# Eight expert blocks moved into the last attention batch, with their rows and biases fetched there

## What is computed

```python
qkv = (x @ W_qkv + b_qkv).reshape(B, S, 3, H, hd)
attn = softmax(einsum('bqhd,bkhd->bhqk', q, k) / sqrt(hd))
attn_out = einsum('bhqk,bkhd->bqhd', attn, v)
gate = softmax(x @ W_gate + b_gate)
top_g, top_i = top_k(gate, 2)
combine = sum(one_hot(top_i, E) * top_g)
expert_out = einsum('bsd,edf->bsef', x, W_experts) + b_experts
moe_out = einsum('bsef,bse->bsf', expert_out, combine)
return attn_out + moe_out        # added to x by the caller
```

## Time and profile before

| what | before |
|---|---|
| median of 3 runs | 1406.44 us (1406.14 to 1407.71) |
| profiled execution, span | 1410.6 us |
| PE busy | 1305.5 us (93%) |
| DVE busy | 967.5 us (69%) |
| ACT busy | 903.4 us (64%) |
| POOL busy | 363.8 us (26%) |
| DMA | 219.83 MB, mean 156 GB/s |

### The profile page before, as it was taken

One profiled execution on the slowest core, in us unless ns is written; L12 is line 12 of the kernel. 1 busy time (PEld: TensorE's weight loads), 2 busy tenths in 40 slices (PEclk: granted clock), 3 DMA queues, 4 the chain that ended last, 5 costly groups with the idle time before them and its releaser, 6 DMA issues. The chain is left out here.

```text
span 1410.6 us, 27655 instructions
## 1 busy us (share of the span) xinstructions
PE 1305.5 (93%) x7744; PEld 994.7 (71%) x7745; DVE 967.5 (69%) x2143; ACT 903.4 (64%) x1888; POOL 363.8 (26%) x572
## 2 busy tenths in 40 slices
PE   4998999999888899999999999999988779999996
PEld 4967888888666567776777776777764358777775
DVE  4256888888678888888888888888876524433332
ACT  4123545444358799999999999999987723333332
POOL 0002222222200011312102131110010047777765
PEclk9998999999899999999999999999996789999998
DMA  5006777776665257564545745556479377867763
GB/s 163 1 1 228 265 268 264 251 266 246 231 164 150 38 135 161 134 165 85 145 128 138 188 84 123 143 144 164 104 166 309 131 191 140 146 124 134 139 129 52
DMA packets 113387, 219.83 MB, mean 156 GB/s; under 512 B 28489, under 2 KB 36809, under 8 KB 111155
## 3 DMA queue, kind: packets, MB, share of 16 engines
q1 hardware_dynamic: 84064, 173.47, 40.9%
q0 software_dynamic: 26624, 42.04, 17.3%
q10 hardware_dynamic: 2643, 3.65, 0.8%
HBM read 86.82 MB, written 77.73 MB: 117 GB/s over the span
## 5 line engine op out<-in xcount | busy, mean ns | idle before, releaser
L225 PE MATMUL banks<-parts 128*128 128x512 f32 (+6 forms) x1108 | 443.0, 400 | 32.7 <-DVE parts L1334 7.4
L227 PE MATMUL banks<-parts 128*128 128x512 f32 (+6 forms) x1108 | 423.5, 382 | 0.0
L226 PE MATMUL banks<-parts 128*128 128x512 f32 (+6 forms) x1108 | 422.9, 382 | 0.0
L1549 DVE TENSOR_REDUCE plain<-banks 128x1 f32<-128x512 f32 x512 | 339.5, 688 | 82.9 <-PE banks L1053 69.8
L774 ACT ACTIVATE banks<-banks,plain 128x512 f32<-128x512 f32 x512 | 346.2, 683 | 15.4 <-DVE plain L1549 15.1
L781 ACT ACTIVATE plain<-banks 128x1024 f32<-128x1024 f32 x256 | 266.9, 1043 | 39.6 <-PE banks L1075 38.4
L225 PEld LDWEIGHTS banks<-parts 128*128 128x128 f32 (+1 forms) x1108 | 214.2, 193 | 85.4 <-issue 24.2
L227 PEld LDWEIGHTS banks<-parts 128*128 128x128 f32 (+1 forms) x1108 | 213.0, 192 | 40.8
L226 PEld LDWEIGHTS banks<-parts 128*128 128x128 f32 (+1 forms) x1108 | 214.4, 194 | 30.8
L1075 PE MATMUL banks<-parts 104*128 104x512 f32 x512 | 179.8, 433 | 6.2 <-ACT plain L781 4.7
L1053 PE MATMUL banks<-parts 96*128 96x512 f32 x512 | 184.9, 413 | 0.7 <-ACT banks L774 0.3
(11 more groups left out here) (180 smaller groups left out, 1506.8 us busy)
## 6 DMA issues: line engine op xcount, KB each, us to landing
parts<-parts SPq DMA_DIRECT2D x384, 128.0 KB, 2.4
parts<-h_turned SPq DMA_DIRECT2D x46, 512.0 KB, 6.5
experts_split<-parts SPq DMA_DIRECT2D x32, 512.0 KB, 4.1
h_turned<-parts SPq DMA_DIRECT2D x32, 512.0 KB, 2.9
parts<-experts_split SPq DMA_DIRECT2D x8, 2048.0 KB, 9.8
plain<-in_x_dram SPq DMA_DIRECT2D x32, 256.0 KB, 4.1
plain<-in_L_ffn_W_experts_dram SPq DMA_DIRECT2D x32, 256.0 KB, 4.1
out_dram<-plain SPq DMA_DIRECT2D x32, 256.0 KB, 2.8
```

Source lines behind the costliest of these rows:

```text
L225: pe.matmul(out, stat[0], mov[0], start=first, stop=False)
L226: pe.matmul(out, stat[0], mov[1], start=False, stop=False)
L227: return pe.matmul(out, stat[1], mov[0], start=False, stop=last)
L1549: dve.tensor_reduce(nmx[:, k, t:t + 1], bank[SB[t]][:], AX.X, ALU.max, negate=True).then_inc(q["f_max"], 1)
```

## The change

In heads 5 to 15 of the last batch the table `FILLED` stands in for `STEP`. The empty `D` slots take the halves of 8 early expert blocks (token `x`, all with expert 0). The tokens `r`, `g` and `l` are the rows' transposes (PE), high part (ACT) and low part (DVE). DVE adds the bias (`early_sum`), POOL multiplies by the gate (`weigh`). POOL gathers blocks 0 to 7 and then 8 to 15 in this batch. The expert stage computes blocks 8 to 71, with gathers 8 blocks ahead; the adds of the first 8 blocks are still made after the attention's outputs have landed. Biases for block 8 to 15 are loaded ahead from a copy in DRAM. Since rows and biases take areas of experts 7 and 6, those two are loaded when blocks 8 to 15 are done, and 3, 4 and 5 as heads 12, 14 and 16 are turned.

```diff
+            "begun": {"pe": "n@1 T2@2 S0 S1 r S2 Pa Pb T0@1 S3 D0",
+                      "act": "t2@2 E3@1 g E0 o t0@1 E1 E2",
+                      "dve": "s@1 n@1 m0 l m1 D1@1 m2 m3"},
...
+        FILLED_FROM = 5
...
-            for token in STEP[KINDS[k % 4]][engine].split():
+            for token in (FILLED if last and k >= FILLED_FROM else STEP)[KINDS[k % 4]][engine].split():
...
+                    if last and of is b and half[0] in "NV":
+                        if what[0] == "D":
+                            yield "x", of, early_half(head, what[1])
+                        continue
...
+                if r == 0:
+                    sp.dma_start(be_early[:], b_exp[bass.ds(e, 1)].broadcast_to([P, D])).then_inc(q["in_wk"], 16)
...
-                    load_expert(3)
...
+                    sp.dma_start(be_first, be_dram.broadcast_to([P, NE * D])).then_inc(q["in_wq"], 16)
+                    sp.wait_ge(q["f_t_full"], T * (NH * b + 12))
+                    load_expert(3)
+                    sp.wait_ge(q["f_t_full"], T * (NH * b + 14))
                     load_expert(4)
-                    sp.wait_ge(q["f_t_full"], T * (NH * b + 12))
+                    sp.wait_ge(q["f_t_full"], T * (NH * b + NH))
+                    sp.wait_ge(q["v_full"], NT + U)
                     load_expert(5)
...
+            for i in range(U, 2 * U):
+                added(i)
+            sp.wait_ge(q["m_tr"], U)
+            load_expert(7)
+            sp.wait_ge(q["m_sum"], U)
+            load_expert(6)
...
+                if i >= 2 * U:
+                    pool.wait_ge(q["m_tr"], i - 2 * U + 1)
+                elif i >= U:
+                    pool.wait_ge(q["h_tr"], NT + i - U + 1)
...
+            def weigh(i):
+
+                pool.wait_ge(q["x1_part"], NT + i + 1)
+                pool.tensor_scalar(rows[i], rows[i], lst[:, i, 1:2], None, ALU.mult).then_inc(q["x1_ready"], 1)
...
+            for i in range(U):
+                fetch(U + i)
+                if i == 4:
+                    attended(B - 1, 0)
+                if i:
+                    weigh(i - 1)
             attended(B - 1, 1)
+            weigh(U - 1)
...
             for i in range(NB):
-                if i + 4 < NB:
-                    fetch(i + 4)
+                if 5 <= i < U + 5:
+                    fetch(2 * U + i - 5)
+                if 2 * U <= i < NB - U:
+                    fetch(i + U)
                 add(i)
...
+            def early_turn(i, k):
+
+                pe.wait_ge(q["f_pt"], ((B - 1) * NH + k - 2) * 2 + 2)
+                pe.wait_ge(q[in_rows(i)], rows_before(i) + 16)
+                for c in range(C):
+                    last = pe.transpose(bank[0][:, c * P:(c + 1) * P], rows[i][:, c * P:(c + 1) * P], ident[:])
+                last.then_inc(q["h_tr"], 1)
...
                         elif what[0] == "T":
+                            if held:
+
+                                pe.wait_ge(q["hT_ready"], NT + held)
+                                held = 0
...
-                    await_ge(dve, "m_done", i - 3)
+                    if part != "first" or k >= 4:
+                        dve.wait_ge(q["m_done"], i - 3)
```

155 lines of the change are left out of this document (118 added, 37 removed), and 6 rows, old and new, of the table FILLED.

## The result

The changed kernel takes 1397.28 us (median of 10 runs, 1392.4 to 1401.23), the one before 1406.38 (median of 10 in the same comparison). The ratio is 0.9935, 95% interval 0.9916 to 0.9953: 9.1 us less, where 19.1 were forecast. The time lies in the forecast's range; the gain is half of what was said.

What follows compares the result with a forecast made beforehand. The last batch was held to be bound by PE's lowered clock, the expert stage by POOL's queue, with PE nearly as tight. Terms -3.5 - 21.6 + 5 + 1 = -19.1 us took 1406.4 to 1387; range 1374 to 1402.

Steps and rivals of the forecast that it cites:

- The expert stage: POOL's queue behind the landing: 237.5 us before loads, 21.6 less than 259.1, with 8.9 of waits for late rows gone.
- rival 1: Expert stage shrinks with its blocks, 64 for 72: 28.8 us less, loads hidden, 1374 us; chance 12%.
- Loads of experts 7 and 6: 4 MB loaded inside the expert stage, sharing DMA packets one for one with gathers and adds: 5 us more, bounds 0 and 13.4.
- near 0: Price of the expert stage's two loads if DMA turns let many small descriptors by; 1382 us in the end.
- Dense adds: Some 10 expert-stage adds without a gather, 1.9 us apart, might be slowed by DMA: 1 us more, bounds 0 and 7.
- rival 2: DMA binds the expert stage: loads cost 13.4 us in full and dense adds 7, 1402 us; chance 15%.
- The landing: Last attention output's landing follows the load's issue, not the batch's end: 0.7 of the 4.2 us gained is lost.
- The tail: Head 15 to last output: two faster products with V give 3.3 us, a half block costs 1.4: 1.9 less of 19.4.
- The last batch: Heads 5 to 14 at 57.0 instead of 59.3 us, 2.3 less, and the tail 1.9 less: 4.2 less.
- What batch 6 doesn't have is 8 x 0.5 = 4.0 on PE.: Last batch, heads 5 to 14: full batch 6 takes 52.3 us; eight blocks' transposes add 4.0, all on the path.
- Rival 3: Last batch: turned scores wait for transposes and both splits, 14.2 us instead of 4.7, 1397 us; chance 10%.
- Rival 4: Last batch: PE still pauses and filled matmuls run at half clock, 27 us more, 1414 us; chance 8%.

Runs made afterwards that it cites:

- e7_noload: The changed kernel with the loads of experts 7 and 6 left out but for 16 columns each: 1393.90 us, ratio 0.9911 to before.
- after: The changed kernel itself in its first profile, against the kernel before: 1397.28 us, ratio 0.9935.
- e4_load0: The changed kernel with expert 0's 2 MB load issued at the start of the last batch, ahead of V and the list of rows: 1389.65 us, ratio 0.9888.
- e16_load0_again: The kernel of e4_load0 unchanged, run again on another chip beside e17_turn_again: 1392.06 us, ratio 0.9920.
- e11_after: The changed kernel itself run again, with a second profile, on another chip: 1395.90 us, ratio 0.9945.
- e17_turn_again: The kernel of e13_turn_later2 unchanged, run again on another chip: 1385.54 us, ratio 0.9875.
- e8_split_first: e4_load0 with ACT's turned exponentials and high part moved ahead of other exponentials in two kinds of heads: 1389.02 us, ratio 0.9891.
- e9_both_early: e8_split_first with DVE's low part also one place earlier: 1390.37 us, ratio 0.9904.
- e3_bank2: The changed kernel with early blocks' transposes in the projections' bank instead of bank 0, turned scores no longer waiting for the splits: 1400.88 us, ratio 0.9972.
- e12_turn_later: e4_load0 with PE's turned scores first in a head, transposes one score later, and ACT's turned exponentials first: 1393.36 us, ratio 0.9909.
- e2_no_product: The changed kernel without the 96 matmuls of the 8 early blocks; turning, splits and waits stay: 1406.98 us, ratio 1.0023.
- e14_best: e13_turn_later2 with the biases and expert 5 (2 MB each) requested only after the first 8 adds have landed: 1392.92 us, ratio 0.9908.
- e1_no_turn: The changed kernel without the early blocks' transposes, splits and the waits for them; the 96 matmuls stay: 1385.12 us, ratio 0.9863.
- e6_late: The changed kernel with the biases and expert 5 (2 MB each) requested only after the first 8 adds have landed: 1395.66 us, ratio 0.9926.
- e10_all: e9_both_early with the two 2 MB transfers requested after the first 8 adds, as in e6_late: 1390.23 us, ratio 0.9903.
- e13_turn_later2: e12_turn_later with ACT's high part one exponential earlier: 1395.58 us, ratio 0.9922.

## Why the forecast was wrong, point by point

1. **The expert stage: right, and a little better than said.** The count of POOL's queue gave 237.5 without the loads; `e7_noload` measured 235.1. The reason given, that the 8.9 us of waits for late rows go when gathers are 8 ahead, fits the traces: outside block 1 and the expert switches, POOL's adds wait 8.7 us in the first profile of before (beyond the usual gap), 4.9 in `after`, of which 4.7 are the two adds beside the loads, and nothing in `e7_noload`. The stage did not shrink by 28.8 as in rival 1.
2. **Loads of experts 7 and 6:** forecast 5, measured 5.2 to 5.7 in the profiles and 4.8 by ratios. The counting one for one fits: in `after` from 1205 to 1216 us, while the loads pass, q1 has 241 packets and POOL's queue 187, and the 256 packets of the loads take 14.6 us where 13.4 were counted. That adds in flight cover part of the backlog was not measured by itself. The Trainium skill (DMA: Bandwidth & Descriptors, on arbitration) says that an engine drains a whole packet of descriptors from one queue before it switches. That holds for both queues, the load's too, so the rule does not by itself let the small ones by, and the "near 0" that the prediction drew from it does not follow; counts of a few microseconds over 16 engines can't tell turns of one from longer turns on both sides.
3. **Dense adds:** forecast 1 of 0 to 7, measured nothing (1.86 us from add to add). With this and the price of the loads rival 2, at 1402, did not occur.
4. **The landing:** 0.7 more forecast, 0.5 more measured. The reason given, that the landing follows the loads and not the batch's end, fits: for one and the same kernel a longer tail came with a shorter landing (`e4_load0` 13.9 and 14.3, `e16_load0_again` 15.9 and 12.5).
5. **The tail:** 1.9 less forecast; it went from 17.0 and 19.4 to 13.9. The clock is 1.00 there, where the before profiles have 0.80 and 0.65, and the forecast counted only the two products with V.
6. **The last batch: here the forecast failed, by 12.7 us in all**, +8.5 where it had -4.2. Two steps of it are wrong.
   - *"POOL's 8 gathers instead of 4 at the batch's start ... are in its idle time."* POOL's time is idle there, but the gathered rows now have a reader in head 5, and the transfer queue of expert 0's load stands beside them. Before, nobody read these rows until more than 80 us later. Price: 7.2 us (`e4_load0` against `e11_after`), of which 4.1 are more idle time of PE (a wait of 4.9 for the rows, in place of one of 0.7 for the bank) and the rest goes with the lower clock, 0.74 in head 5 against 1.00. I had followed the moved gathers on POOL's queue and not on the DMA engines, though the earlier trace rows shows these at 0.70 in the empty heads and 235 GB/s.
   - *"What batch 6 doesn't have is 8 x 0.5 = 4.0 on PE."* PE's busy time was right within 1 us (56.9 against 55.9). The step took the work for the time. Each set of transposes uses bank 0, which the exponentials of the turned scores leave 0.7 to 1.5 us too late: 8.3 us (`e4_load0`). With the transposes later it is 3.4 (`e17_turn_again`).
   - Together: 7.2 for the rows, 65.2 - 59.8 = 5.4 for heads 5 to 14 without that, 0.2 ahead of head 5, and 4.3 less in the tail: 8.5.
7. **Rival 3 had the size and not the mechanism.** It gave 1397. It named the splits as the chain, but in after PE has no wait for these, and making them sooner moved nothing that can be measured (`e8_split_first`, `e9_both_early`). The wait is on the other side of the transposes, for the bank to come free. Where the splits do bind is `e3_bank2`, and in part the kernels whose wait for the bank is already shorter (2.7 us in `e12_turn_later`). Over half of the miss, 7.2 of 12.7 us, comes from the late rows, which no rival had; that the total came out at rival 3's 1397 is chance.
8. **Rival 4, the clock,** did not occur: 0.95 in heads 5 to 14. All that is missing is in head 5 (0.64 in `after`, behind the pause; 0.74 in `e11_after`, behind the wait for rows); in heads 6 to 14 it is 1.00, with seven waits of 0.7 to 1.4 us. `e2_no_product` shows what the filled matmuls do for it: without them the waits grow to 25.4 us, the clock in heads 5 to 14 is 0.74 and the whole gain is gone. The second failure mode that the Trainium skill describes (TensorE: Matmul & The Clock Gate), a clock that swings because of small pauses between groups of matmuls, fits that run, not the changed kernel.
9. **Baseline.** The forecast was made against an execution that was 4 us longer in heads 3 and 4 than the other two of before. Subtracting 4.2 for the median set that right by luck. In the changed kernel that pause costs nothing, since without it head 5 waits for the rows: heads 3 to 5 take 24.8 us with it and 24.6 without (`e11_after`).

**Open:** what the pause in heads 3 and 4 is. It was in 5 of 20 profiled executions (the first of before, after, and all three of one chip), and `e3_bank2` has 8.7 us in head 4 alone with named waits. That the kernel alone doesn't cause it is shown, by the same kernel with it and without on two chips; what does is not, nor whether it goes with the chip or with the execution, since no kernel was profiled twice on one chip. Nor was it tried to remove the last 3.4 us at the transposes, or to put the late transfers of `e14_best` onto a chip without the pause.

## What to carry to other kernels

Filling idle slots of an engine is free only where the inputs are there and their buffer is free at that very slot: for each operation that is moved ask who last held its bank or buffer, and when its data lands beside the transfers of that new place. A transfer that is moved forward gets a reader that is nearer; follow it on the DMA engines, not only on the queue that issues it. And fill slots with matmuls even where they save little, if the alternative is a PE that pauses: here the clock was worth more than the 96 matmuls cost (`e1_no_turn`, `e2_no_product`). And compare versions on one chip: across two, the same kernel differed by 10 us.

## What the runs showed of the hardware

- Taking 96 matmuls out of the last batch made it longer: 79.8 instead of 72.2 us for heads 5 to 14, at a granted clock of 0.74 and 0.95 there (`e2_no_product`, `e11_after`).
- Two 2 MB transfers beside it doubled the time from the issue of a 512 KB output to the first instruction after its landing: 14.2 us against 6.7 (`e11_after`, `e6_late`). Moved away, they cost 4 to 7 us at their new place (`e6_late`, `e10_all`, `e14_best`).
- A transfer of 74 KB in 9216 pieces of 8 bytes filled the DMA engines for about 5 us, and a 2 MB load issued behind it on the same queue had its packets only after it (`after`, 1034 to 1039 us).
- PE, ACT and DVE stood still together for 3.5 us in `e13_turn_later2`, with no wait in the trace that explains it, while POOL went on issuing. It decided between two versions until both had run on one chip without it: 1395.58 and 1385.54 us for the same kernel, with before at 1406.42 and 1403.44.
